# A second attention layer on one core: both halves of a round's scores issued together, the values a round later and first, the accumulators copied out by ScalarE

## What is computed

```python
h = N_HEAD                               # 8
qh = q.reshape(b * h, d // h, m)         # 16 channels, 256 queries
kh = k.reshape(b * h, d // h, -1)
vh = v.reshape(b * h, c // h, -1)
scale = 1.0 / jnp.sqrt(jnp.asarray(d // h, dtype=q.dtype))
qk = jnp.einsum('bdm,bdn->bmn', qh, kh) * scale
sm = jax.nn.softmax(qk, axis=-1)
ret = jnp.einsum('bmn,bcn->bcm', sm, vh)
```

## Time and profile before

| | |
|---|---|
| median of 3 runs | 1830.45 us (1828.95 to 1835.7) |
| the profiled execution, its own time | 1835.48 us |
| its span, first to last instruction | 1833.7 us |
| busy over the span: PE, DVE, ACT, POOL | 1525.9, 1080.1, 804.5, 794.2 us |
| mean granted clock of PE | 0.871 of full speed |
| the second attention layer, first score to last add | 474.8 to 572.83 us |

### The profile page before, as it was taken

One profiled execution on the slowest core, in us unless ns is written; L12 is line 12 of the kernel. 1 busy time (PEld: TensorE's weight loads), 2 busy tenths in 40 slices (PEclk: granted clock), 3 DMA queues, 4 the chain that ended last, 5 costly groups with the idle time before them and its releaser, 6 DMA issues. The chain is left out here.

```text
span 1833.7 us, 25059 instructions
## 1 busy us (share of the span) xinstructions
PE 1525.9 (83%) x8562; PEld 980.8 (53%) x8600; DVE 1080.1 (59%) x2317; ACT 804.5 (44%) x1879; POOL 794.2 (43%) x959
## 2 busy tenths in 40 slices
PE   7566659999797799997399999999799989836772
PEld 5222235656464365655167777777455555525661
DVE  7999961223674643355778888888722255462336
ACT  3989862110333211112488888888521112412221
POOL 3367641000200299791277777777210000027772
PEclk9655659999697999998699999999899988858796
DMA  2499871110504011320200000000111100156656
GB/s 78 89 177 182 172 162 33 36 42 18 184 2 167 27 48 65 115 66 25 68 2 1 1 1 1 1 1 1 44 30 43 35 25 1 46 195 233 231 171 238
DMA packets 174223, 140.12 MB, mean 76 GB/s; under 512 B 141793, under 2 KB 154721, under 8 KB 170386
## 3 DMA queue, kind: packets, MB, share of 16 engines
q1 hardware_dynamic: 165314, 114.89, 22.0%
q0 software_dynamic: 6416, 22.03, 3.6%
q10 hardware_dynamic: 2368, 1.61, 0.3%
HBM read 85.43 MB, written 19.50 MB: 57 GB/s over the span
## 5 line engine op out<-in xcount | busy, mean ns | idle before, releaser
L389 PE MATMUL l1e_gu<-x_normT,l1e_w 128*128 128x512 f32 x384 | 171.6, 602 | 0.0
L1859 POOL CAST l0m_pi<-l0m_pf 128x1024 bf16<-128x1024 int16 x128 | 133.2, 1040 | 87.0 <-ACT l0m_pf L1926 85.4
L1451 PE MATMUL l2x_pr<-l_w,l2x_xq 128*128 128x512 bf16 x538 | 133.6, 385 | 37.8 <-ACT credits L42 35.9
L1926 ACT ACTIVATE l0m_pf<-l0m_s,l0m_bias,l0x_sq 128x1024 int16<-128x1024 f32 x128 | 153.9, 1204 | 19.2 <-DVE l0m_bias L1957 12.6
L1953 DVE TENSOR_REDUCE l0m_mx<-l0m_s 128x1 f32<-128x1024 f32 x128 | 155.6, 1215 | 4.7 <-PE l0m_s L1868 4.4
L1868 PE MATMUL l0m_s<-l0x_kT,l0x_qT 64*128 64x512 bf16 x256 | 70.6, 575 | 64.7 <-ACT l0m_pf L1926 63.5
L389 PE MATMUL l0e_gu<-x_normT,l0e_w 128*128 128x512 f32 x272 | 121.3, 601 | 0.0
L1578 DVE BATCH_NORM_STATS2 l2x_bn<-l2x_raw 128x6 f32<-128x128 f32 x384 | 83.3, 279 | 64.3 <-ACT l2x_raw L1519 64.3
L389 PEld LDWEIGHTS l1e_gu<-x_normT,l1e_w 128*128 128x128 f32 x384 | 74.2, 194 | 84.2 <-issue 83.1
L389 PE MATMUL l2e_gu<-x_normT,l2e_w 128*128 128x512 f32 x256 | 114.3, 602 | 0.0
L441 ACT ACTIVATE l1e_sil<-l1e_gu 128x512 f32<-128x512 f32 x48 | 28.6, 596 | 178.6 <-PE l1e_gu L389 178.6
(11 more groups left out here) (505 smaller groups left out, 3608.1 us busy)
## 6 DMA issues: line engine op xcount, KB each, us to landing
l3m_w<-in_l_moe SPq DMA_DIRECT2D x16, 1280.0 KB, 6.9
l1e_w<-in_l_ffn SPq DMA_DIRECT2D x24, 384.0 KB, 3.1
l_rows<-zero_row SPq DMA_DIRECT2D x8, 1024.0 KB, 10.9
l_w<-l_rows SPq DMA_DIRECT2D x8, 1024.0 KB, 12.7
l0e_w<-in_l_ffn SPq DMA_DIRECT2D x17, 384.0 KB, 3.1
l2e_w<-in_l_ffn SPq DMA_DIRECT2D x16, 384.0 KB, 3.1
ctx_tok<-l_route SPq DMA_DIRECT2D x8, 512.0 KB
l2q_wps<-in_l_wp SPq DMA_DIRECT2D x16, 256.0 KB, 2.8
```

What stands on the lines that cost most here:

```text
L389: last = nc.tensor.matmul(gu[half][:, m, :], w[:, c % SW, (2 * k + m) * P:(2 * k + m + 1) * P], pg.xnT[:, k, cols(n)], start=(k == 0), sto ...
L1451: last = nc.tensor.matmul(flat(pr[t % 2][:]), src[:, k, tokens], pg.l2_w3[:, part, k, at:at + W], start=(k == 0 and part == 0), stop=(k == ...
L1859: nc.gpsimd.tensor_copy(pi[:, n % 8, :], pf[:, n % 4, :]).then_inc(s["rounded"], 1)
L1926: nc.scalar.activation(pf[:, n % 4, :], s_ps[n % 3][:], ACT.Exp, scale=sq[:, h, b:b + 1], bias=bias[:, n % 4:n % 4 + 1], accum_out=sm[:, b ...
```

## The change

It does five things, all in `attention_l1`:

- PE's loop issues `value(i - 3)` first, then `turn_max(i - 1)`, `score(i, 0)`, `score(i, 1)`, `shift(i - 1, 0)`, `shift(i - 1, 1)`. It has 19 iterations in place of 18. `uses` is not changed.
- `pT` has three buffers in place of two, and the exponentials wait for the values of three rounds ago.
- A new step on ACT, `read_output(b)`, copies both halves of `po` (128x512) to the new SBUF tile `oS` ahead of round `2 * b + 3`'s exponentials; the next sample's values wait for this copy (`o_read`) where they waited for the product (`scaled`).
- `scale(b)` reads `oS` in place of `po`, and `rec` has two buffers.
- DVE's loop issues `augment(i - 1)` first, then `scale`, then both maxima.

```diff
--- before.py
+++ after.py
@@ -755,8 +755,8 @@
     nc, H, C = pg.nc, 8, 16
     Q = 2 * B
     sems = ("const", "masks", "qm_in", "cb_in", "vz_in", "scores", "maxed", "nm_turned", "augmented", "shifted", "exped", "pv",
-            "recip", "scaled", "added")
-    const, masks, qm_in, cb_in, vz_in, scores, maxed, nm_turned, augmented, shifted, exped, pv, recip, scaled, added = (
+            "recip", "scaled", "added", "o_read")
+    const, masks, qm_in, cb_in, vz_in, scores, maxed, nm_turned, augmented, shifted, exped, pv, recip, scaled, added, o_read = (
         pg.sem(f"l1x_{m}") for m in sems)
     with ExitStack() as st:
         def sb(m, shape, dt=F32):
@@ -773,8 +773,9 @@
         ones = sb("ones", [P, 2, 32])
         nm = sb("nm", [P, 2, KD, P])
         qa = sb("qa", [P, 2, D])
-        pT = sb("pT", [P, 2, 4, KD, D])
-        rec = sb("rec", [P, D])
+        pT = sb("pT", [P, 3, 4, KD, D])
+        oS = sb("oS", [P, 2, 2, D])
+        rec = sb("rec", [P, 2, D])
         on = sb("on", [P, 2, D])
         ring = [psum(f"r{i}", [P, 2, 2 * D]) for i in range(3)]
         nmT = psum("nmT", [P, 2 * D])
@@ -872,7 +873,7 @@
                 b, par = divmod(q, 2)
                 pe.wait_ge(exped, 2 * q + 2)
                 if par == 0 and b >= 1:
-                    pe.wait_ge(scaled, b)
+                    pe.wait_ge(o_read, b)
                 if q == 0:
                     pe.wait_ge(vz_in, 2 + 2 + 2 * KD)
                 for nh in range(KD):
@@ -880,19 +881,18 @@
                         for j in range(4):
                             rows = slice(32 * j, 32 * j + 32)
                             w = vz[:, par, nh, b * P + 32 * j:b * P + 32 * j + 32] if what == 0 else ones[:, par, :]
-                            last = nc.tensor.matmul(po[rows, what, :], w, pT[:, par, j, nh, :], start=(par == 0 and nh == 0 and what == 0),
+                            last = nc.tensor.matmul(po[rows, what, :], w, pT[:, q % 3, j, nh, :], start=(par == 0 and nh == 0 and what == 0),
                                                     stop=(par == 1 and nh == 1), skip_group_check=True)
                 last.then_inc(pv, 1)
 
-            for i in range(Q + 2):
-                if i < Q:
-                    score(i, 0)
+            for i in range(Q + 3):
+                if 0 <= i - 3 < Q:
+                    value(i - 3)
                 if 0 <= i - 1 < Q:
                     turn_max(i - 1)
                 if i < Q:
+                    score(i, 0)
                     score(i, 1)
-                if 0 <= i - 2 < Q:
-                    value(i - 2)
                 if 0 <= i - 1 < Q:
                     shift(i - 1, 0)
                     shift(i - 1, 1)
@@ -904,13 +904,21 @@
                 for par in range(2):
                     nc.scalar.activation(cb[:, par, half, :], pg.ctxt[:, half, :], ACT.Identity, scale=own[:, par:par + 1],
                                          bias=other[:, par:par + 1]).then_inc(cb_in, 1)
-            for q in range(Q):
-                for pr in range(2):
+            def read_output(b):
+                act.wait_ge(pv, 2 * b + 2)
+                if b >= 2:
+                    act.wait_ge(scaled, b - 1)
+                nc.scalar.activation(oS[:, b % 2].rearrange("p a d -> p (a d)"), po[:].rearrange("p a d -> p (a d)"), ACT.Copy).then_inc(o_read, 1)
+
+            for q in range(Q + 2):
+                if q >= 2 and q % 2 == 1 and q - 3 >= 0:
+                    read_output((q - 3) // 2)
+                for pr in range(2 if q < Q else 0):
                     act.wait_ge(shifted, 2 * q + pr + 1)
-                    if q >= 2:
-                        act.wait_ge(pv, q - 1)
+                    if q >= 3:
+                        act.wait_ge(pv, q - 2)
                     ps = ring[slot_of["t", q, pr] % 3]
-                    nc.scalar.activation(pT[:, q % 2, 2 * pr:2 * pr + 2].rearrange("p j k n -> p (j k n)"),
+                    nc.scalar.activation(pT[:, q % 3, 2 * pr:2 * pr + 2].rearrange("p j k n -> p (j k n)"),
                                          ps[:].rearrange("p j n -> p (j n)"), ACT.Exp).then_inc(exped, 1)
 
         @block.vector
@@ -941,21 +949,20 @@
                 v.tensor_tensor(qa[:, par, :], nmT[:, 0:D], qm[:, par, b, :], ALU.add).then_inc(augmented, 1)
 
             def scale(b):
-                dve.wait_ge(pv, 2 * b + 2)
-                v.reciprocal(rec[:], po[:, 1, :]).then_inc(recip, 1)
-                dve.wait_ge(recip, b + 1)
+                dve.wait_ge(o_read, b + 1)
                 if b >= 2:
                     dve.wait_ge(added, b - 1)
-                v.tensor_tensor(on[:, b % 2, :], po[:, 0, :], rec[:], ALU.mult).then_inc(scaled, 1)
+                v.reciprocal(rec[:, b % 2], oS[:, b % 2, 1, :]).then_inc(recip, 1)
+                dve.wait_ge(recip, b + 1)
+                v.tensor_tensor(on[:, b % 2, :], oS[:, b % 2, 0, :], rec[:, b % 2], ALU.mult).then_inc(scaled, 1)
 
             for i in range(Q + 3):
+                if 0 <= i - 1 < Q:
+                    augment(i - 1)
                 if i >= 4 and i % 2 == 0:
                     scale((i - 4) // 2)
                 if i < Q:
                     top(i, 0)
-                if 0 <= i - 1 < Q:
-                    augment(i - 1)
-                if i < Q:
                     top(i, 1)
```

## The result

The changed kernel takes 1856.13 us (median, 1854.41 to 1863.21) against 1829.97 us before, a ratio of 1.0148 with an interval of 1.0127 to 1.017: slower, as forecast, but by 26 us where 15 were forecast, and 0.1 us above the top of the range.

The account below looks back on a forecast made before the run. PE, busy throughout at full clock, bounded the layer; afterwards its wait for DVE's maximum would. Gaps +16.0, head +1.3, tail -2.3 gave +15.0 us on the 1830.45 median: 1845.5 (+0.8%), own range 1841 to 1852, with rivals 1837 to 1856.

Parts of the forecast that it names:

- The loop: Turn, score, reduction, second shift half and values follow one another in each round: 5.74 us at full clock, against 5.22.
- a scaling round: Every second round, reciprocal and product on DVE delay the first maximum by 1.40 us, making the round 7.14.
- the copy, the third buffer and the SBUF reads: ACT's copy hidden by 0.03 us, third pT buffer costed at nothing, reciprocal from SBUF taken as unchanged.
- The tail: Turn 15 to the last add's end: 9.8 us against 12.14, -2.3, as last shifts no longer queue behind a value.
- A: Rival: PE passes the waiting shift half and begins the values, hiding its wait; 1825 us, not slower; chance 0.07.
- B: Rival: the scaling does not delay the maximum, all 13 gaps take 5.74; 1837 us; chance 0.10.
- The sum: 13 gaps from turn 2 to turn 15: 83.0 us against 67.02, +16.0; with head and tail, +15.0.
- rival C: The clock stays down because PE has gaps every round: 45 us above forecast, 1890, 3.9 per late round; chance 0.07.
- The head: Layer's start at half clock: turn 0 to 1 unchanged, turn 1 to 2 takes 9.6 us against 8.29, +1.3.
- two late rounds of C: The clock's rise coming two rounds late, at 3.9 us each; the range reached up over this to 1856.

Follow-up runs that it names:

- the order alone: Kernel before with only the change's order of PE and DVE: two pT buffers, no copy by ACT, scaling out of PSUM; ratio 1.0119.
- the scaling last: Changed kernel with one move on DVE, the scaling behind both maxima instead of ahead of them; ratio 1.0035.
- the products elsewhere: Changed kernel with three idle 128x256 products in each scaling round, behind the second shift half where PE does not wait; ratio 1.0148.
- one product: Changed kernel with one idle 128x256 product between the two shift halves of each scaling round; ratio 1.0111.
- the pause filled: Changed kernel with three idle 128x256 products between the two shift halves of each scaling round, where PE waits; ratio 1.0072.
- the values cut in two: Changed kernel with scaling behind both maxima and the values in two halves, one ahead of the scores, one behind the turn; ratio 0.9938.

## Why the prediction was right and wrong

**The loop: right.** 5.74 was forecast for a plain round, 5.76 is there; 7.14 for a scaling round, 7.14 is there. PE's waits are 0.47 and 1.85 us, the two sizes that were named (0.4 and 1.8). That the copy, the third buffer and the SBUF reads carry nothing is borne out: the copy takes 598 ns where the earlier trace rows had 597, the reciprocal 1.74 where the earlier trace rows had 1.76, and the order alone gives the same gaps. The tail is right to 0.1.

**Rivals A and B: wrong, as weighed.** PE's order let nothing past the waiting half, and the scaling did delay the maximum, by 2.94 - 1.55 = 1.39 for 1.40. The kernel with the scaling last is what B would have looked like: 5.76 in twelve gaps.

**The clock: this step failed.** The sum put falls of the clock inside the loop at nothing, and they cost 11.4 us. The prediction set rival C at 0.07, with the sentence "Against it: from 560 to 574 PE was busy for only 6.09 of 14 us and the clock stayed at 1.00, and my loop is busier than either". It took the busy share of one tail for evidence about a loop. In the changed kernel the stretches at 1.00 between falls are busier than that tail (7.88 of 10.20 us), and each ends in a fall all the same. What the falls go with is the pause in the scaling rounds: in the three profiles with the change's order and nothing in the pause (two of the changed kernel, one of the order alone), 14 of 18 pauses of 1.85 us had one, which began between 0.2 us before PE's restart and 1.2 us after it. Without the pause and with the same wait for DVE there was none, and with the pause and the same added work elsewhere there were three. With the scaling last, PE's work in two rounds is that of the changed kernel (10.59 and 10.58 us), the long pause is gone, and so are the falls.

The Trainium skill, "TensorE: Matmul & The Clock Gate" (section "A second HAM failure mode: psum-queue depth-cycling"), was cited for just this, a clock that swings between its levels because PE idles briefly between groups; the trace after agrees with it, with five falls, and that of the kernel run again with six. By that rule the time was to lie somewhere between 1845 and 1890 (the prediction says "layer" there and means the kernel), and 1856 is there. What made PE idle here was the wait for DVE's maximum. The price in the prediction was also too coarse. C was reckoned as rounds that stay at half clock, at 3.9 each; a fall here costs 1.6 or 3.2, as part of one round runs slow. The forecast's 83.0 plus five falls, 11.4, is the measured 94.5 to within 0.1.

**The head: the size was off, with either sign.** +1.3 was forecast, from a rise of the clock at the end of the first values. In the profile of the result the rise came sooner and the head gave -1.35; in the changed kernel run again it took the forecast's 9.6. When the clock rises in the head belongs to the execution, and the range should have had 2.65 us for it. The range's upper end held two late rounds of C, 7.8 us, where the falls cost 11.4. That the layer of the result is only 8.9 us above the forecast's is in part luck of this head: run again, with the head as forecast and six falls, it was 14.8 above.

**What stays open.** The runs do not tell whether the length of the single pause counts or the share of the loop in which PE is busy. The two go together here: in two undisturbed rounds PE is busy for 10.58 of 12.89 us in the changed kernel, 12.08 of 14.39 with the products elsewhere and 11.21 of 12.89 with one product, all three with falls, and for 12.08 of 12.89 with the pause filled and 10.59 of 11.52 with the scaling last, both without. No run has a long pause at a high share, or many short ones at a low share. Nor do they tell which of the pauses bring a fall: 4 of 18 did not, and neither did those of 1.64 and 2.01 us at the end of the layer before, where the clock stayed up to 573.9. And the part behind the layer, which no kernel changes, varies by up to 9.5 us between these profiles; the 2.3 us of the medians' difference that are not in the layer may lie there.

## What to carry to other kernels

When an order of work makes an engine pause that was busy throughout, price the pause twice: for itself, and for what the clock loses behind it. Do not take the mean busy share of another stretch for evidence that the clock holds in a loop; look for the loop's longest pauses, and put what their falls may cost into the sum and the range. If the pause can't be removed, other useful work of the same engine belongs in it, as with the values cut in two; even idle products bought back 8 us here (layer 121.89 to 113.55).

## What the runs showed of the hardware

At pauses of TensorE of 1.85 us (14 of 18) and of 1.22 us (5 of 6) the granted clock fell from 1.00 to 0.50 for 3.4 or 6.8 us at a time, though in the changed kernel the engine was busy for over 75% of each stretch at 1.00 between two falls; with pauses of 0.47 us in every round, over 85 us, it did not fall. In the kernel before, eight idle products raised the clock 20 us sooner (471.8 for 491.95) but for 6.9 us only: it fell inside the second of the first round's waits of 1.34 and 2.40 us, and the layer took 98.08 us for 98.04.
